# One of four sums over states accumulated by TensorE in PSUM, with a decay factor moved from PSUM to SBUF

## The chip, the cores and the metric

The kernel runs on one core of one Trainium2 chip. The metric is device time in microseconds (us) of one execution, and the number given for a kernel is the median of its runs. Everything is in fp32.

## The reference, cut to what matters

The program computes four residual layers over 2 x 2048 tokens of width 256. The change touches only the first one, a state-space (Mamba) layer; a mixture of experts, a channel mix, an attention and a second mixture of experts follow it and stay as they are.

```python
xm, z = split(x @ W_in.T)                 # ED = 512 channels each
xc    = silu(conv(xm) + conv_b)
dt, Bm, Cm = split(xc @ W_xproj.T)        # Bm and Cm have N = 16 states
delta = softplus(dt @ W_dt.T + b_dt)
dA    = exp(delta[..., None] * A)         # the decay factor, per channel and state
dBx   = delta[..., None] * Bm * xc[..., None]
h     = dA_t * h + dBx_t                  # a scan over time, per channel and state
y     = einsum('ben,bn->be', h, C_t)      # the sum over the 16 states
y     = (y + D_skip * xc) * silu(z);  out = y @ W_out.T
```

The change concerns the last sum: for every token and channel, 16 products of h and C are added up.

## The kernel before, in words

The state-space stage (`mamba_phase`) works through 8 blocks of T = 512 tokens ("units"), two to a pass of a hardware loop (`hf` = 0 and 1). In a unit the loop `for n in range(NS)` goes over the 16 states. Channels lie on partitions, in EC = 4 groups of 128; time is the free dimension. One step n of one unit, which the text calls **state n**, is:

- POOL: two `product` instructions (L400) make dBx for state n+1 in the buffer `hs[(n+1) % 4]`, 128x1024 each.
- ACT: four `factor` instructions (L554) make the decay factors of state n+1, one channel group each, in the PSUM banks `dA0` to `dA3`.
- DVE: four `scan` instructions (L778) run h = dA * h + dBx over time, reading the bank `dA[c]` and the SBUF tile `hs`, and writing h into `hs`.
- PE: four `turn`s (L924) of four 128x128 transposes each bring h of state n-1 into two PSUM banks `hT_ps` (token tile j = 0 and 2 in the one, 1 and 3 in the other), so that tokens lie on partitions and C is a number per partition.
- The four token tiles are four running sums `acc[:, j, :]` of 128x512. Tiles 0 and 2 are summed by DVE straight from PSUM (`summed`, L743). Tiles 1 and 3 (`OFF`) go another way: ACT scales them into the SBUF tile `part` (`weighted`, L568) and POOL adds `part` to `acc` (`add`, L412).

Work of state n's `turn`, `weighted`, `summed` and `add` belongs to h of state n-1: the last sum of a unit is finished in state 0 of the next. What a unit needs besides is put between the turns by two tables written by hand: `EARLY[n]` stands between turn 1 and turn 2 of state n on PE, `LATE[n]` after turn 3. Among these tasks are `y0` to `y3` of the unit before (`output`, L843 and L845, which read `acc`), `o0`, `o1`, the convolution `xc0` to `xc3` of the next unit (states 3 to 8), `dt` (state 9), `d0` to `d3` (10 and 11), `z0` to `z3` (11 to 13) and the router `r` (14). Each engine takes its instructions in order; semaphores tie them together. A wait on PE or ACT therefore holds all that stands behind it. All eight PSUM banks are taken: four `dA`, two `hT_ps`, and `fx` and `fy` for the tasks.

## Time and profile before

| | us |
|---|---|
| median of 3 runs | 2560.29 |
| lowest and highest run | 2547.91 and 2561.58 |
| the profiled execution, its own time | 2548.84 |
| span of its trace | 2547.0 |
| busy: PE, DVE, POOL, ACT | 1965.9, 1714.8, 1429.0, 1149.4 |
| mean granted TensorE clock | 0.844 |

The state-space stage takes about the first 1200 us of the span and repeats itself every 136.5 us, once for a unit. Everything below is read from one unit in the middle (about 354 to 490 us), whose picture returns in the others. The trace gives for a group of instructions its busy time and the mean of one; a timeline merges equal instructions that follow one another; where an engine sat idle, brackets give for how long and what ended it. One fp32 matmul is two matmul records.

### The profile page before, as it was taken

What the parts mean: (1) busy time and instruction counts of PE and PEld (TensorE: products, weight loads), DVE (VectorE), ACT (ScalarE), POOL (GpSimd) and SP (SyncE); (2) the same over time, 40 slices, a digit from 0 to 9 for tenths busy, and PEclk for the clock granted to TensorE, in tenths of its full rate; (3) what the DMA queues carried; (4) which work ended last, traced back from release to release, by engine and by line L of the source; (5) the groups of instructions that cost most, each with busy time, mean ns of one, the idle gap of its engine ahead of it and who ended that gap; (6) DMA issues with size and microseconds to landing.
All of it is one profiled execution on the core that took longest, in us unless ns stands there. A gap on an engine that the chain in (4) does not pass through costs nothing. (4 is left out here: it accounts for less than half of the span.)

```text
span 2547.0 us, 35987 instructions
## 1 busy us (share of the span) xinstructions
PE 1965.9 (77%) x10324; PEld 1506.0 (59%) x10325; DVE 1714.8 (67%) x3375; ACT 1149.4 (45%) x1895; POOL 1429.0 (56%) x1002
## 2 busy tenths in 40 slices
PE   6787868696978787786499999904978986599980
PEld 2445555454645454545399999803665665499970
DVE  1788788888888888885744444376943786644438
ACT  2676767677676867673223232212501442111112
POOL 1789899999989898985133333221300220255542
PEclk9897879696978888786599999956987887699995
DMA  2111111111111010111411111151000002222216
GB/s 73 34 34 47 34 47 34 46 34 44 38 34 44 28 52 30 50 34 34 205 48 48 47 47 47 39 178 35 0 17 11 9 25 90 107 71 69 69 55 197
DMA packets 77371, 139.14 MB, mean 55 GB/s; under 512 B 10449, under 2 KB 48465, under 8 KB 76450
## 3 DMA queue, kind: packets, MB, share of 16 engines
q1 hardware_dynamic: 63586, 100.19, 11.7%
q0 software_dynamic: 13632, 37.24, 4.6%
q8 instruction: 55, 0.90, 0.1%
q14 instruction: 98, 0.80, 0.1%
HBM read 105.38 MB, written 32.01 MB: 54 GB/s over the span
## 5 line engine op out<-in xcount | busy, mean ns | idle before, releaser
L778 DVE TENSOR_TENSOR_SCAN a_hs<-a_dA,a_carry,a_hs 128x512 f32<-128x512 f32 x512 | 637.1, 1268 | 27.8 <-POOL a_hs L400 23.8
L400 POOL TENSOR_TENSOR a_hs<-a_u,a_b_bc 128x1024 f32<-128x1024 f32 x258 | 625.2, 2426 | 0.4
L924 PE MATMUL a_h_ps<-k_ident,a_hs 128*128 128x128 f32 x2064 | 341.1, 318 | 184.5 <-DVE a_hs L778 113.7
L924 PEld LDWEIGHTS a_h_ps<-k_ident,a_hs 128*128 128x128 f32 x2064 | 284.6, 165 | 303.4 <-DVE a_hs L778 136.5
L554 ACT ACTIVATE a_dA<-a_delta,a_a_neg 128x512 f32<-128x512 f32 x512 | 351.7, 688 | 105.5 <-DVE a_hs L778 103.1
L412 POOL TENSOR_TENSOR a_acc<-a_acc,a_part 128x512 f32<-128x512 f32 x242 | 324.4, 1341 | 70.2 <-ACT a_part L568 69.0
L743 DVE SCALAR_TENSOR_TENSOR a_acc<-a_h_ps,a_c_tok,a_acc 128x512 f32<-128x512 f32 x242 | 177.3, 733 | 110.7 <-PE a_h_ps L924 110.6
L568 ACT ACTIVATE a_part<-a_h_ps,a_c_tok 128x512 f32<-128x512 f32 x242 | 165.7, 685 | 149.4 <-PE a_h_ps L924 133.2
L1224 POOL DMA_INDIRECT expert_rows<-m0e_ys,k_pair x71 | 74.1, 1044 | 236.2 <-DVE m0e_ys L1280 225.1
L1290 DVE TENSOR_TENSOR m0e_hT<-m0e_gs,m0e_u 128x512 f32<-128x512 f32 x70 | 48.1, 688 | 186.9 <-ACT m0e_gs L1243 186.9
L1243 ACT ACTIVATE m0e_gs<-m0e_g 128x512 f32<-128x512 f32 x71 | 42.4, 597 | 269.7 <-PE m0e_u L1321 269.7
L1247 ACT ACTIVATE m1e_hT<-m1e_u 128x512 f32<-128x512 f32 x71 | 42.4, 597 | 227.5 <-PE m1e_u L1321 227.5
L859 PE MATMUL a_fx<-a_hT,a_w_x 128*128 128x512 f32 x288 | 135.5, 606 | 7.9 <-ACT a_halo L490 7.9
L1270 DVE TENSOR_SCALAR m1e_xT<-m1e_x,k_ln_w,k_ln_b 128x128 f32<-128x128 f32 x142 | 51.7, 406 | 132.4 <-PE m1e_x L1309 119.7
L1321 PE MATMUL m1e_u<-m1e_xT,m1e_wu 128*128 128x128 f32 x1136 | 140.2, 277 | 0.5 <-DVE m1e_wu L1274 0.4
L1321 PE MATMUL m0e_g<-m0e_xT,m0e_wg 128*128 128x128 f32 x1136 | 140.1, 277 | 0.0
L1321 PE MATMUL m0e_u<-m0e_xT,m0e_wu 128*128 128x128 f32 x1136 | 139.5, 276 | 0.0
L1321 PEld LDWEIGHTS m1e_u<-m1e_xT,m1e_wu 128*128 128x128 f32 x1136 | 134.1, 194 | 1.2 <-issue 1.1
L1331 PE MATMUL m0e_y<-m0w_down,m0e_hT 128*128 x568 | 134.5, 380 | 0.2 <-DVE m0e_ys L1280 0.2
L1321 PEld LDWEIGHTS m0e_g<-m0e_xT,m0e_wg 128*128 128x128 f32 x1136 | 134.2, 194 | 0.1
L1331 PE MATMUL m1e_y<-m1w_down,m1e_hT 128*128 x568 | 134.2, 379 | 0.0
L1321 PEld LDWEIGHTS m0e_u<-m0e_xT,m0e_wu 128*128 128x128 f32 x1136 | 133.7, 193 | 0.0
(427 smaller groups left out, 3785.1 us busy)
## 6 DMA issues: line engine op xcount, KB each, us to landing
a_b_bc<-b_rows SPq DMA_DIRECT2D x132, 256.0 KB, 3.1
q_y<-expert_rows SPq DMA_DIRECT2D x32, 512.0 KB, 5.6
a_xl<-in_L_attn_x SPq DMA_DIRECT2D x9, 512.0 KB, 3.4
norm_rows<-a_shared SPq DMA_DIRECT2D x9, 512.0 KB, 2.9
m0w_up<-in_m_up SPq DMA_DIRECT2D x1, 4096.0 KB, 12.3
m0w_gate<-in_m_gate SPq DMA_DIRECT2D x1, 4096.0 KB, 22.2
m0w_down<-in_m_down SPq DMA_DIRECT2D x1, 4096.0 KB, 32.3
q_xl<-in_L_attn_x SPq DMA_DIRECT2D x8, 512.0 KB, 3.5
```

Source lines behind the costliest of these rows:

```text
L400: pool.tensor_tensor(hs[n % NBUF][:, half, :], u[s][:, half, :], b_bc[:, n % NBUF:n % NBUF + 1, :].broadcast_to([P, 2, T]), ALU.mult).then ...
L412: pool.tensor_tensor(acc[s][:, j, :], acc[s][:, j, :], part[:, j // 2, :], ALU.add).then_inc(s_add, 1)
L554: act.activation(dA[c][:], delta[s][:, c, :], ACT.Exp, scale=a_neg[:, c, k:k + 1]).then_inc(s_da, 1)
L568: act.activation(to, hT_ps[j % 2][:], ACT.Copy, scale=c_tok[s][:, j, k:k + 1]).then_inc(s_part, 1)
L743: dve.scalar_tensor_tensor(out=acc[s][:, j, :], in0=hT_ps[j % 2][:], scalar=weight, in1=acc[s][:, j, :], op0=ALU.mult, op1=ALU.add).then_i ...
L778: dve.tensor_tensor_scan(hs[k][:, c, :], dA[c][:], hs[k][:, c, :], carry[:, hf, c, n:n + 1], ALU.mult, ALU.add).then_inc(s_scan, 1)
L859: last = pe.matmul(ps[:], w_x[:, q, d, k * P:(k + 1) * P], hT[:, d, q:q + T], start=q == 0 and d == 0, stop=q == KC - 1 and d == DC - 1)
L924: last = pe.transpose(hT_ps[j % 2][:, c * P:(c + 1) * P], hs[(n - 1) % NBUF][:, c, j * P:(j + 1) * P], ident[:])
L1224: pool.indirect_dma_start(io["expert_rows"], bass.IndirectOffsetOnAxis(ap=per.pair[:, s:s + 1], axis=0), ys[s % 2][:], None).then_inc(s_st ...
L1270: last = dve.tensor_scalar(xT[k][:, c, :], x_ps[:, c, :], scale[:, c:c + 1], shift[:, c:c + 1], ALU.mult, ALU.add)
L1321: last = pe.matmul(ps[k][:, f, :], w[k][:, c, f * P:(f + 1) * P], xT[k][:, c, :], start=c == 0, stop=c == DC - 1)
L1331: last = pe.matmul(y_ps[k][:], hT[k][:, c, :], w_down[:, c, bass.ds(e * D, D)], start=c == 0, stop=c == FC - 1)
```

## The change

PSUM has eight banks and all were taken. The change frees one by keeping the decay factor of channel group 3 in an SBUF tile (`dA_sb`), so that the fourth scan reads two SBUF tiles. The freed bank (`sum_ps`) takes the sum of token tile 3 (`PILED`): ACT still scales the tile into `part`, but PE then multiplies `part` by the identity matrix and accumulates in the bank (`pile`, one fp32 matmul of 128x128 by 128x512 for each state), in place of POOL's `add`. Once for each unit ACT copies the finished sum into `acc` (`copy_sum`), and `y0` waits for that copy. Tile 1 (`ADDED`) stays with ACT and POOL, and POOL has one `add` in a state instead of two. Neither table of tasks is changed.

```diff
-        dA = [m.ps(f"dA{c}", [P, T]) for c in range(EC)]
+        dA = [m.ps(f"dA{c}", [P, T]) for c in range(EC - 1)] + [m.sb("dA_sb", [P, T])]
+        sum_ps = m.ps("sum", [P, ED])
...
-        ND, NO, ADDS = len(ON), len(OFF), len(OFF) * (NS - 1)
+        ND, NO, ADDS = len(ON), len(OFF), NS - 1
+        ADDED, PILED = OFF
...
             def add(U, n, j, s):
 
-                if j not in OFF or n == 1:
+                if j != ADDED or n == 1:
                     return
...
+            def copy_sum(U, s):
+
+                act.wait_ge(s_sum, piled(U, 0))
+                act.activation(acc[s][:, PILED, :], sum_ps[:], ACT.Copy).then_inc(s_sumc, 1)
+
             def weighted(U, n, j, s):
...
+                if j == PILED:
+                    act.wait_ge(s_sum, piled(U, n - 1))
+                    to = part[:, j // 2, :]
+                elif n == 1:
                     to = acc[s][:, j, :]
...
                         weighted(U, n, 1, here)
+                        if n == 1:
+                            copy_sum(U, 1 - hf)
                         factor(U, n + 1, 0, there)
...
                     if whole == "y0":
                         pe.wait_ge(s_acc, lin(U, NS * ND, 2 * ND))
-                        pe.wait_ge(s_add, lin(U, ADDS, 2 * NO))
+                        pe.wait_ge(s_add, lin(U, ADDS, 2))
+                        pe.wait_ge(s_sumc, lin(U, 1, 1))
...
+            def pile(U, n):
+
+                pe.wait_ge(s_part, part_count(U, n, PILED))
+                if n == 1:
+                    pe.wait_ge(s_sumc, lin(U, 1, 1))
+                pe.matmul(sum_ps[:], ident[:], part[:, PILED // 2, :], start=n == 1, stop=n == 0).then_inc(s_sum, 1)
...
                         turn(U, n, 0)
                         turn(U, n, 1)
+                        if n != 1:
+                            pile(U, n - 1)
                         for name in EARLY.get(n, []):
                             task(name, U, F, 1 - hf)
                         turn(U, n, 2)
                         turn(U, n, 3)
+                        if n == 0:
+                            pile(U, 0)
                         for name in LATE.get(n, []):
                             task(name, U, F, 1 - hf)
```

After the loop the last unit's sum is finished in the same way; the closing y of channel group 3 uses the bank `sum_ps`.

On PE, in a state of the convolution (state 5; a_hs0 to a_hs3 are the four buffers of h, a_h_ps the transposed tile, a_fy the bank of the convolution task), there stands before:

```order
L924 MATMUL a_h_ps0<-k_ident,a_hs0 128x128 [waits a_scan]
L924 MATMUL a_h_ps0<-k_ident,a_hs0 128x128 x3
L924 MATMUL a_h_ps1<-k_ident,a_hs0 128x128 [waits a_weighted_by_act]
L924 MATMUL a_h_ps1<-k_ident,a_hs0 128x128 x3
L859 MATMUL a_fy<-a_hT,a_w_x 128x512 x2
```

and after the change, at the same place:

```order
L945 MATMUL a_h_ps0<-k_ident,a_hs0 128x128 [waits a_scan]
L945 MATMUL a_h_ps0<-k_ident,a_hs0 128x128 x3
L945 MATMUL a_h_ps1<-k_ident,a_hs0 128x128 [waits a_weighted_by_act]
L945 MATMUL a_h_ps1<-k_ident,a_hs0 128x128 x3
L953 MATMUL a_sum<-a_part,k_ident 128x512 [waits a_weighted_by_act]
L879 MATMUL a_fy<-a_hT,a_w_x 128x512 x2
```

Nothing has moved but the pile (L953), which stands ahead of the convolution's matmuls, and the convolution, turn 2 and turn 3 come one matmul later.

On PE at the end of state 0 and in state 1, up to the task y0 (a_fy here), there stands before:

```order
L924 MATMUL a_h_ps<-k_ident,a_hs 128x128 [waits a_weighted_by_act]
L924 MATMUL a_h_ps<-k_ident,a_hs 128x128 x3
L918 REGISTER_ALU
L922 REGISTER_ALU [waits a_summed_by_dve]
L924 MATMUL a_h_ps<-k_ident,a_hs 128x128 [waits a_scan]
L924 MATMUL a_h_ps<-k_ident,a_hs 128x128 x3
L924 MATMUL a_h_ps<-k_ident,a_hs 128x128 [waits a_weighted_by_act]
L924 MATMUL a_h_ps<-k_ident,a_hs 128x128 x3
L896 ISA
L903 ISA [waits a_summed_by_dve,a_y_task_free]
L843 MATMUL a_fy<-a_xc,a_diag_d 128x512 [waits a_summed_by_pool]
```

and after the change:

```order
L945 MATMUL a_h_ps<-k_ident,a_hs 128x128 x3
L950 REGISTER_ALU
L953 MATMUL a_sum<-a_part,k_ident 128x512 [waits a_weighted_by_act]
L943 REGISTER_ALU [waits a_summed_by_dve]
L945 MATMUL a_h_ps<-k_ident,a_hs 128x128 [waits a_scan]
L945 MATMUL a_h_ps<-k_ident,a_hs 128x128 x3
L945 MATMUL a_h_ps<-k_ident,a_hs 128x128 [waits a_weighted_by_act]
L945 MATMUL a_h_ps<-k_ident,a_hs 128x128 x3
L916 ISA
L923 ISA [waits a_summed_by_dve,a_y_task_free]
L924 ISA [waits a_summed_by_pool]
L863 MATMUL a_fy<-a_xc,a_diag_d 128x512 [waits a_sum_copied]
```

Between turn 3 of state 0 and turn 0 of state 1 there is now a pile that waits for ACT's `weighted` of that very state, and y0 waits for ACT's copy as well.

On POOL, in one state, there stands before (a_hs is the product, a_acc the add):

```order
L400 TENSOR_TENSOR a_hs<-a_u,a_b_bc 128x1024 [waits a_b_loaded0]
L407 REGISTER_ALU
L411 REGISTER_ALU [waits a_weighted_by_act]
L412 TENSOR_TENSOR a_acc<-a_acc,a_part 128x512 [waits a_summed_by_pool]
L400 TENSOR_TENSOR a_hs<-a_u,a_b_bc 128x1024
L407 REGISTER_ALU
L411 REGISTER_ALU [waits a_weighted_by_act]
L412 TENSOR_TENSOR a_acc<-a_acc,a_part 128x512 [waits a_summed_by_pool]
```

and after the change:

```order
L409 TENSOR_TENSOR a_hs<-a_u,a_b_bc 128x1024 [waits a_b_loaded0]
L416 REGISTER_ALU
L420 REGISTER_ALU [waits a_weighted_by_act]
L421 TENSOR_TENSOR a_acc<-a_acc,a_part 128x512 [waits a_summed_by_pool]
L409 TENSOR_TENSOR a_hs<-a_u,a_b_bc 128x1024
```

The second add is gone, and the two products of neighbouring states follow each other directly.

## Rows read from the trace of the kernel before

**Rows 1.** The page's costliest groups (busy us, mean ns of one, idle before).

```profile
L778 DVE TENSOR_TENSOR_SCAN a_hs<-a_dA,a_carry,a_hs 128x512 f32<-128x512 f32 x512 | 637.1, 1268 | 27.8 <-POOL a_hs L400 23.8
L400 POOL TENSOR_TENSOR a_hs<-a_u,a_b_bc 128x1024 f32<-128x1024 f32 x258 | 625.2, 2426 | 0.4
...
L554 ACT ACTIVATE a_dA<-a_delta,a_a_neg 128x512 f32<-128x512 f32 x512 | 351.7, 688 | 105.5 <-DVE a_hs L778 103.1
...
L568 ACT ACTIVATE a_part<-a_h_ps,a_c_tok 128x512 f32<-128x512 f32 x242 | 165.7, 685 | 149.4 <-PE a_h_ps L924 133.2
```

**Rows 2.** Busy time by stretch: states 6, 10, 11, 12 and 15.

```profile
403.12:410.02 6.90, 6.90 (x30) 3.92 (x29) 6.12 (x7) 4.42 (x8) 6.90 (x5) 1.00 0.10 36
...
435.53:443.30 7.77, 4.51 (x23) 2.70 (x22) 7.73 (x16) 5.95 (x11) 7.72 (x5) 0.96 0.13 44
443.30:453.80 10.50, 10.50 (x29) 5.71 (x28) 6.22 (x8) 9.53 (x14) 6.01 (x5) 0.54 0.09 28
453.80:465.83 12.03, 6.91 (x32) 3.95 (x30) 12.03 (x11) 10.16 (x15) 11.57 (x8) 0.89 0.09 22
...
483.49:490.60 7.11, 3.85 (x18) 3.14 (x16) 6.34 (x9) 4.05 (x7) 7.11 (x5) 0.50 0.24 84
```

The columns are the stretch, its length, busy us (and count) of PE, PEld, DVE, ACT and POOL, the granted clock, the DMA share and GB/s.

**Rows 3.** Timeline of PE in state 6 (start, us, engine).

```profile
402.48 1.04 PE L924 MATMUL a_h_ps<-k_ident,a_hs 128*128 128x128 f32 x8
403.35 1.88 PE L859 MATMUL a_fx<-a_hT,a_w_x 128*128 128x512 f32 x4
405.07 1.04 PE L924 MATMUL a_h_ps<-k_ident,a_hs 128*128 128x128 f32 x8
405.94 3.60 PE L859 MATMUL a_fx<-a_hT,a_w_x 128*128 128x512 f32 x8
409.38 1.04 PE L924 MATMUL a_h_ps<-k_ident,a_hs 128*128 128x128 f32 x8
```

**Rows 4.** Timeline of POOL in the same state.

```profile
406.08 2.36 POOL L400 TENSOR_TENSOR a_hs<-a_u,a_b_bc 128x1024 f32<-128x1024 f32 x1
408.40 1.27 POOL L412 TENSOR_TENSOR a_acc<-a_acc,a_part 128x512 f32<-128x512 f32 x1
409.62 2.36 POOL L400 TENSOR_TENSOR a_hs<-a_u,a_b_bc 128x1024 f32<-128x1024 f32 x1
...
413.16 2.37 POOL L400 TENSOR_TENSOR a_hs<-a_u,a_b_bc 128x1024 f32<-128x1024 f32 x1
```

**Rows 5.** What PE waited for in the stage (us in total, times, longest).

```profile
PE a_fy L843 <- POOL a_acc L412: 22.2, 8, 3.2
```

**Rows 6.** Timeline of PE from state 0 to y0.

```profile
359.81 2.30 PE L924 MATMUL a_h_ps<-k_ident,a_hs 128*128 128x128 f32 x8 [2.23 <-DVE a_hs L778]
364.62 2.08 PE L843 MATMUL a_fy<-a_xc,a_diag_d 128*128 128x512 f32 x2 [2.51 <-POOL a_acc L412]
```

**Rows 7.** Timeline of ACT over the same stretch.

```profile
360.28 0.66 ACT L568 ACTIVATE a_part<-a_h_ps,a_c_tok 128x512 f32<-128x512 f32 x1
...
362.23 0.69 ACT L568 ACTIVATE a_acc<-a_h_ps,a_c_tok 128x512 f32<-128x512 f32 x1
```

**Rows 8.** Timeline of PE in state 11.

```profile
443.84 2.07 PE L872 MATMUL a_fx<-a_dbc,a_w_dt 64*128 64x512 f32 x2
445.71 1.91 PE L872 MATMUL a_fy<-a_dbc,a_w_dt 64*128 64x512 f32 x2
447.55 1.97 PE L924 MATMUL a_h_ps<-k_ident,a_hs 128*128 128x128 f32 x8
```

**Rows 9.** DVE operations with two SBUF inputs (ns, min/median/max).

```profile
L684 DVE SCALAR_TENSOR_TENSOR a_acc<-a_acc,a_u x18: 1196/2290/2395, 68.5 to 1139.3; 128x1024 f32<-128x1024 f32 x18
```

**Rows 10.** POOL's add over the stage (ns, min/median/max).

```profile
L412 POOL TENSOR_TENSOR a_acc<-a_acc,a_part x242: 1254/1272/2353, 87.1 to 1177.8; 128x512 f32<-128x512 f32 x121
```

**Rows 11.** Timeline of POOL in state 12.

```profile
455.77 2.21 POOL L412 TENSOR_TENSOR a_acc<-a_acc,a_part 128x512 f32<-128x512 f32 x1
457.95 3.32 POOL L400 TENSOR_TENSOR a_hs<-a_u,a_b_bc 128x1024 f32<-128x1024 f32 x1
```

**Rows 12.** Timeline of DVE in state 12.

```profile
455.66 3.41 DVE L684 SCALAR_TENSOR_TENSOR a_acc<-a_acc,a_u 128x1024 f32<-128x1024 f32 x2
```

More of the change, by code:

```diff
@@ L227, in mamba_phase @@
         s_add = m.sem("summed_by_pool")
+        s_sum = m.sem("summed_by_pe")
+        s_sumc = m.sem("sum_copied")
         s_carry = m.sem("carry")
@@ L286, in part_count, with piled @@
             return lin(U, NS * NO, NO * n + OFF.index(j) + 1 + NO)
+        def piled(U, n):
+            return lin(U, NS, n + 2)
         def added_count(U, n, j):
-            return lin(U, ADDS, NO * (n - 1 if n > 1 else 0) + OFF.index(j) + 1 + NO)
+            return lin(U, ADDS, (n - 1 if n > 1 else 0) + 2)
         ROWS = R + 2 * NS
         N_WEIGHTS = 16 * 11
-        N_PREP = 1 + EC + 8
+        N_PREP = 1 + EC + 9
         PER_D = 2 * (2 + 2)
@@ L370, in _ @@
             pool.memset(xc[1][:], 0.0).then_inc(s_prep, 1)
+            pool.memset(part[:, PILED // 2, :], 0.0).then_inc(s_prep, 1)
             pool.memset(H[:, BT - TJ:BT, :], 0.0).then_inc(s_prep, 1)
-            pool.sem_inc(s_add, NO)
+            pool.sem_inc(s_add, 1)
             pool.wait_ge(s_const, 2)
@@ L408, in add @@
                 if n == 0:
-                    pool.wait_ge(s_add, added_count(U, 0, j) + -NO)
+                    pool.wait_ge(s_add, added_count(U, 0, j) + -1)
                 elif n > 2:
@@ L446, in _ @@
             end = (0, 2 * NB, None)
-            for j in OFF:
-                add(end, 0, j, 1)
+            add(end, 0, ADDED, 1)
             rms(TILES - TJ, lambda per_: per_ * (2 * NB + 1))
@@ L561, in weighted @@
                 k = (n - 1) % NS
-                if n == 1:
+                if n == 1 and j == OFF[0]:
                     act.wait_ge(s_free[side("ct")], count("ct", before(U)))
+                if j == PILED:
+                    act.wait_ge(s_sum, piled(U, n - 1))
+                    to = part[:, j // 2, :]
+                elif n == 1:
                     to = acc[s][:, j, :]
                 else:
-                    act.wait_ge(s_add, added_count(U, 0, j) + -NO if n == 0 else added_count(U, n - 1, j))
+                    act.wait_ge(s_add, added_count(U, 0, j) + -1 if n == 0 else added_count(U, n - 1, j))
                     to = part[:, j // 2, :]
@@ L651, in _ @@
                 weighted(end, 0, j, 1)
+            copy_sum(end, 1)
             act.wait_ge(s_free["Y"], len(FSEQ["Y"]) + 2 * NB * len(SEQ["Y"]) + 2)
@@ L823, in _ @@
                 dve.wait_ge(s_yl, c + 1)
-                dve.tensor_tensor(z[1][:, c, :], dA[c][:], z[1][:, c, :], ALU.mult).then_inc(s_yg, 1)
+                dve.tensor_tensor(z[1][:, c, :], (dA[0:EC - 1] + [sum_ps])[c][:], z[1][:, c, :], ALU.mult).then_inc(s_yg, 1)
             t_end = TILES - TJ
@@ L932, in _ @@
             pe.wait_ge(s_prep, N_PREP)
+            pe.matmul(sum_ps[:], ident[:], z[1][:, 0, :], start=True, stop=False)
             with pe.Fori(0, NB) as i:
@@ L948, in _ @@
                 turn(end, 0, j)
+                if j == 1:
+                    pile(end, -1)
+            pile(end, 0)
             pe.wait_ge(s_acc, lin(end, NS * ND, 2 * ND))
-            pe.wait_ge(s_add, lin(end, ADDS, 2 * NO))
+            pe.wait_ge(s_add, lin(end, ADDS, 2))
+            pe.wait_ge(s_sumc, 2 * NB + 1)
             pe.wait_ge(s_da, 2 * NB * NS * EC + EC)
+            last_y = dA[0:EC - 1] + [sum_ps]
             for c in range(EC):
-                output(dA[c], c, 1).then_inc(s_yl, 1)
+                output(last_y[c], c, 1).then_inc(s_yl, 1)
             pe.wait_ge(s_yg, EC)
```

## Prediction

> **What bounds the kernel now.** I read the page's costliest groups first, then a table of busy times by state for one unit, then the timelines of PE, POOL, DVE and ACT in the states that the table singled out. The groups [rows 1] show POOL's two products at 2.4 us each and DVE's four scans at 1.27 us as the largest work of the stage; that alone suggests that POOL, which also has two adds, sets the pace. The table [rows 2] says more. In state 6, one of the convolution's, POOL is busy for 6.90 of 6.90 us, but so is PE, at a granted clock of 1.00, while DVE has 6.12. State 15 has POOL full (7.11 of 7.11), PE at 3.85. State 11 has PE full (10.50 of 10.50) and POOL at 6.01. State 12 has DVE full (12.03). So the bound changes inside a unit, and an add taken from POOL is worth something only in the states where POOL alone is full: 15, 0 and half of 14. The reader is to see in the timeline of PE [rows 3] that in a convolution state turn, matmul, turn, matmul stand back to back with no wait in brackets: 402.48 to 409.38 is 6.90 us, the length of the state. States 4 to 8 look so.
>
> **What is removed.** One add of 1.27 us, which takes 1.22 us of POOL's sequence (408.40 to 409.62 [rows 4]). POOL's state is 7.08 us (406.08 to 413.16 [rows 4]) and becomes 5.86. Where POOL alone is the bound the next limit is DVE, 6.34 us in state 15 [rows 2]: at most 0.74 us a state, 2.5 states, 1.8 us a unit. PE's wait for POOL's last add ahead of y0 goes too: 22.2 us in 8 units, 2.8 each [rows 5]; what takes its place is worked out below.
>
> **The pile in states 4 to 8.** It is one fp32 matmul of 128x512, two records. Four such records fill 403.35 to 405.07 [rows 3], 0.43 us each, so a pile is 0.86 us of a full PE. Nothing covers it: PE has no wait in these states. From 6.90 a state goes to 7.76, while POOL falls below. Five states: **+4.3 us a unit**. Elsewhere (states 2, 3, 9, 10, 12, 13, 15) PE waits between its turns and the pile lies in that wait; without this cover each would cost 0.86 us too.
>
> **States 0 and 1.** The pile after turn 3 of state 0 waits for ACT's `weighted` of the same turn. In the trace that one runs late, 360.28 to 360.94 [rows 7], because four layer-norm instructions stand ahead of it on ACT. The turns of state 1 started at 359.81 [rows 6]. Behind the waiting pile they now start after 360.94 and a pile. The clock is 0.50 here (state 15 in [rows 2]); at such a clock two records take 1.87 us (443.84 to 445.71 [rows 8]). So: pile done at 362.8, eight transposes of 1.97 [rows 8] to 364.8, `weighted` 0.7, the copy 0.7 (nearest row: the same shape from PSUM, 685 ns [rows 1]), y0 at 366.4, against 364.62 [rows 6]: **+1.8 us a unit**. Bounds: at the full clock (0.86 for the pile, 1.04 for the turns [rows 3]) y0 starts at 364.4, -0.2; if DVE's sum of state 1, behind the delayed turn 0, decides instead, the whole shift of the turns, 362.8 less 359.81, +3.0.
>
> **State 11.** PE is full, at a clock of 0.54 [rows 2], and ACT's evacuation of d2 and d3 waits for it. The pile stands ahead of d2: **+1.9 us a unit** by [rows 8], 0.9 at the full clock.
>
> **The fourth scan and the SBUF port.** Scans with dA in PSUM have one SBUF tensor input and show no disturbance: their mean is 1268 ns beside a busy POOL [rows 1]. No scan of this kernel reads two SBUF tiles, so its behaviour beside POOL has to be bounded from other operations. DVE's scalar_tensor_tensor with two SBUF inputs has a minimum of 1196 ns and a median of 2290 [rows 9]: 1.09 us is waiting. At the same moment (two of them, 455.66 for 3.41 us [rows 12]) POOL's add takes 2.21 us instead of 1.27 and its product 3.32 instead of 2.36 [rows 4, 10, 11], each 0.95 us longer. Each engine waits for the other's instruction to end. The fourth scan should do this in every state: it waits up to 1.1 us for POOL, and POOL loses 1.27 less the 0.25 that the pairs overlap (1.20 against 0.95), 1.0 us. In a state where POOL is full its 5.86 becomes 6.87, against 7.08: the gain is 0.2 and not 0.74, over 2.5 states **-0.5 us a unit**. In states 2, 10, 12, 13 and 14 DVE or what waits for it decides, and scan 3 is followed by turn 0 of the next state; there the wait counts. POOL is busy for 7.72 of 7.77 us in state 10 and 11.57 of 12.03 in state 12 [rows 2], with less to do after the change; I take 0.6 us, about half of the 1.09 seen: **+3.0 us a unit**. Bounds: 0 if the scan takes no port from POOL, 5.5 if it waits for 1.09 in each. In states 4 to 8 DVE has 0.8 us to spare now and 1.6 then, which hides the wait.
>
> The Trainium skill, page "SBUF — State Buffer", section "Who interferes with whom", says that VectorE with two SBUF inputs and GpSimd take one shared pair of ports by an exclusive lock, each for the whole instruction. By that rule, the stretched pairs agree, and it speaks against moving the factor to SBUF; without it the unit would be 4.3 us shorter than with it (3.0 less the wait, 1.3 more relief).
>
> **ACT.** Writing the factor to SBUF costs nothing by the rows: 688 ns into PSUM, 685 from PSUM into SBUF [rows 1]. The page "ScalarE: Activation LUTs" of the Trainium skill, section "Step-by-step: what each stage is for", calls ScalarE's way to PSUM the faster one; the two rows do not show it, and the sum leaves it out. The copy adds 0.7 us a unit, counted above.
>
> **Sum.** 4.3 + 1.8 + 1.9 + 3.0 - 0.5 = 10.5 us a unit, 84 us in 8 units. The profiled execution took 2548.84 us, so 2633. The median of the runs stands 11 us above the profiled one and a new median may fall anywhere in that spread; I say **2637**.
>
> **The rivals.**
> - **The scan takes no port.** For it: no scan in the trace shows a lock. Against it: two other operations with two SBUF inputs behave alike. 4.3 + 1.8 + 1.9 - 1.8 = 6.2 a unit, +50: 2598. Chance 0.20.
> - **The clock rises in the slow states.** PE has more to do in states 13 to 1 and in 9 to 11, and the clock may stay at 1.00. For it: the clock is 1.00 in the full states 4 to 8. Against it: it is at 0.54 in state 11 although PE is busy throughout. 4.3 - 0.2 + 0.9 + 3.0 - 0.5 = 7.5 a unit, +60: 2609. Chance 0.15.
> - **Faster: POOL is what sets the pace in the convolution states, and PE has hidden room.** POOL is full there as well [rows 2], and a busy PE is modelled. If PE takes the pile into gaps that the records do not show, and the scan takes no port, the states with a full POOL (4 to 8, 14, 15, 0, 2) fall toward DVE's 6.34: 9 x 0.7 = 6.3 us a unit, -50: 2498. It decides only where a pile in states 4 to 8 costs less than the 0.18 us by which POOL's 7.08 stands above PE's 6.90. Against it: [rows 3] leaves no gap. Chance 0.06.
> - **Nothing measurable.** The port costs little, the clock rises and POOL's relief pays for the convolution states; about 2560. Chance 0.06.
> - **Worse.** The waits for the port chain up: 4.3 + 3.0 + 1.9 + 5.5 = 14.7 a unit, +118: 2666 or more. Chance 0.08 for what lies near or above.
> My own forecast keeps 0.45.
>
> **How the numbers follow.** Lowest bound of each term without a port: 4.3 - 0.2 + 0.9 - 1.8 = 3.2 a unit, +26 us, 2575; highest 2666, and 11 us for the spread of the medians. The range is 2583 to 2672: it leaves out the faster and the unchanged case (0.12) and the ends of the others. A measurement of this kernel can tell about 0.5%, 13 us, from no change. Faster 0.06, same 0.06, slower 0.88.
>
> **What the changed kernel's profile would show.** Right: in states 4 to 8 PE stays full and the state takes 7.7 to 7.8 us, not 6.9; turns of state 1 start about 3 us later against the fourth scan of state 0; the scan that reads the SBUF factor has a mean well above 1268 ns and POOL's products have a maximum of 3.3 us in many states, not only in 12 and 13; a unit takes 147 us, not 136.5. Wrong: a fourth scan of 1.27 us throughout; waits on PE in the convolution states; a granted clock above 0.9 in states 13 to 1; POOL still without idle time in states 4 to 8. The prediction fails upward if DVE waits for POOL in states that I hold to be covered (4 to 9), and downward if the pile is hidden there.

## The result, and the profile after

| | before | after |
|---|---|---|
| median (20 runs each) | 2556.61 us | 2567.70 us |
| lowest to highest | 2547.91 to 2565.89 | 2560.44 to 2581.96 |
| profiled execution, span | 2548.84, 2547.0 | 2570.06, 2568.3 |
| mean granted clock over the span | 0.844 | 0.883 |

The ratio is 1.0050 with a 95% interval of 1.0034 to 1.0065: slower by about 13 us, at the edge of what was called measurable. The forecast was 2637 with a range of 2583 to 2672; the result lies below its range.

The page's costliest groups of after (busy us, mean ns of one, idle before), against [rows 1]:

```profile
L409 POOL TENSOR_TENSOR a_hs<-a_u,a_b_bc 128x1024 f32<-128x1024 f32 x258 | 683.5, 2667 | 1.0 <-issue 0.3
L798 DVE TENSOR_TENSOR_SCAN a_hs<-a_dA,a_carry,a_hs 128x512 f32<-128x512 f32 x384 | 479.8, 1264 | 11.8 <-POOL a_hs L409 8.5
...
L421 POOL TENSOR_TENSOR a_acc<-a_acc,a_part 128x512 f32<-128x512 f32 x121 | 186.8, 1544 | 130.9 <-ACT a_part L585 130.2
...
L798 DVE TENSOR_TENSOR_SCAN a_hs<-a_dA_sb,a_carry,a_hs 128x512 f32<-128x512 f32 x128 | 247.0, 1930 | 0.0
```

Three quarters of the scans are as they were; the fourth takes 1930 ns in the mean, and POOL's product went from 2426 to 2667. POOL now has 130 us of idle time in which it waits for ACT: over the stage as a whole it no longer sets the pace.

PE in state 6 (timeline: start, us), against [rows 3]:

```profile
408.99 1.04 PE L945 MATMUL a_h_ps<-k_ident,a_hs 128*128 128x128 f32 x8
409.86 1.02 PE L953 MATMUL a_sum<-a_part,k_ident 128*128 128x512 f32 x2
410.72 1.88 PE L879 MATMUL a_fx<-a_hT,a_w_x 128*128 128x512 f32 x4
412.44 1.03 PE L945 MATMUL a_h_ps<-k_ident,a_hs 128*128 128x128 f32 x8
413.31 3.60 PE L879 MATMUL a_fx<-a_hT,a_w_x 128*128 128x512 f32 x8
416.75 1.03 PE L945 MATMUL a_h_ps<-k_ident,a_hs 128*128 128x128 f32 x8
```

408.99 to 416.75 is 7.76 us where it was 6.90: the pile's 0.86 us, in full. Busy time by stretch in after (columns as in [rows 2]): states 0, 1, 4, 11 and 12.

```profile
360.01:368.77 8.76, 5.92 (x18) 3.42 (x17) 6.99 (x7) 5.96 (x11) 8.76 (x5) 0.69 0.26 92
368.77:378.39 9.62, 8.27 (x52) 6.19 (x51) 9.02 (x17) 5.05 (x12) 6.16 (x4) 0.94 0.20 55
394.10:401.87 7.77, 7.77 (x32) 4.31 (x31) 6.87 (x7) 4.56 (x8) 6.76 (x4) 1.00 0.10 34
...
451.45:461.31 9.86, 9.21 (x31) 4.44 (x30) 7.26 (x7) 7.32 (x12) 6.86 (x4) 0.81 0.14 34
461.31:473.82 12.51, 8.35 (x36) 4.44 (x36) 12.16 (x11) 12.45 (x17) 8.47 (x6) 1.00 0.06 21
```

State 11, all at 0.54 in [rows 2], is at 0.81 now, and at 1.00 from the middle on: the timeline of PE there, against [rows 8]:

```profile
450.30 1.97 PE L945 MATMUL a_h_ps<-k_ident,a_hs 128*128 128x128 f32 x8 [2.63 <-DVE a_hs L798]
452.06 1.92 PE L953 MATMUL a_sum<-a_part,k_ident 128*128 128x512 f32 x2
453.90 1.77 PE L892 MATMUL a_fx<-a_dbc,a_w_dt 64*128 64x512 f32 x2
455.52 1.02 PE L892 MATMUL a_fy<-a_dbc,a_w_dt 64*128 64x512 f32 x2
```

The pile takes 1.92 us, as forecast; but the clock rises behind it, and the second pair of d takes 1.02 instead of 1.91.

One unit's states differ, so all are compared by one measure: the length of a state from DVE's first sum in it to the first sum of the next, worked out from the timelines of DVE as a mean over units 1 to 6 of 8 (us), and the mean granted clock of the same stretches. The kernels below "after" are those of the experiments: "small outside" has piles of 4 columns outside states 4 to 8, "pairs" is the kernel before with an idle pair in all states, "no port" is that without POOL's second add, "ring" has three banks in rotation, and "fastest" is the last one. Where a state of another kernel is quoted below, it is by the same measure. A clock of 1.00 is 2.4 GHz and one of 0.50 is 1.2 GHz; values between are a mean over both levels.

```
state           unit     0     1     2     3   4-7     8     9    10    11    12    13    14    15
before         136.5  6.68 12.68  8.84  6.86  6.90  8.64  9.78  7.78  9.94 12.49 10.21  7.46  7.52
after          138.3  8.26  9.45  8.88  6.87  7.76  9.50  8.60  8.11  9.87 12.26 10.26  7.78  7.36
factor alone   147.5  8.09 12.78  8.85  7.16  8.00  8.29 10.44  8.69 10.25 13.31 10.47  9.03  8.12
small outside  143.9  7.56 11.45  9.32  7.88  7.69  9.50 10.56  9.05 10.62 11.93 10.15  7.98  7.17
pairs          139.8  6.80 12.78  8.86  8.07  7.76  9.50  8.60  7.78  7.72 13.42 10.18  7.49  7.61
no port        133.2  6.21  9.72  8.85  8.06  7.76  9.50  9.09  7.78  7.72 11.20 10.17  6.44  7.46
ring           138.2  8.27  9.26  8.86  6.86  7.76  9.50  8.60  7.78 11.37 11.67 11.39  6.38  7.28
ring, pair     134.8  8.16  9.65  8.87  6.87  7.76  9.50  9.99  7.77  8.12 10.94 10.21  6.33  7.32
after, pair    142.2  8.02 10.54  8.95  6.88  7.76  9.50  9.75  9.59 10.13 12.33 10.27  7.75  7.42
fastest        130.3  8.32  9.96  8.90  6.86  6.90  8.64  9.46  7.77  8.11 10.94 10.24  6.30  7.17
clock before    0.83  0.50  0.72  1.00  1.00  1.00  1.00  0.86  0.96  0.57  0.91  0.77  0.54  0.50
clock after     0.93  0.72  0.98  1.00  1.00  1.00  1.00  1.00  0.95  0.79  0.96  0.89  0.78  0.74
```

The unit grew by 1.8 us where 10.5 were forecast. States 4 to 8 give +4.3, as forecast; state 0 has +1.6, and states 1 and 9 give back 3.2 and 1.2.

### The profile page after: what moved, and what is told of

It reads as the page before. It is cut to its first block and busy times, and to the rows that moved or that the text cites. A ratio compares the mean times of both kernels' runs of the same rounds, so it can differ in the third digit from the quotient of the medians.

```text
span 2568.3 us, 36192 instructions
## 1 busy us (share of the span) xinstructions
PE 2018.7 (79%) x10586; PEld 1502.8 (59%) x10587; DVE 1788.3 (70%) x3375; ACT 1155.8 (45%) x1904; POOL 1383.0 (54%) x882
## 5 line engine op out<-in xcount | busy, mean ns | idle before, releaser
L409 POOL TENSOR_TENSOR a_hs<-a_u,a_b_bc 128x1024 f32<-128x1024 f32 x258 | 683.5, 2667 | 1.0 <-issue 0.3
L798 DVE TENSOR_TENSOR_SCAN a_hs<-a_dA,a_carry,a_hs 128x512 f32<-128x512 f32 x384 | 479.8, 1264 | 11.8 <-POOL a_hs L409 8.5
L945 PEld LDWEIGHTS a_h_ps<-k_ident,a_hs 128*128 128x128 f32 x2064 | 262.7, 153 | 284.2 <-DVE a_hs L798 146.4
L945 PE MATMUL a_h_ps<-k_ident,a_hs 128*128 128x128 f32 x2064 | 307.6, 297 | 144.5 <-DVE a_hs L798 113.9
L562 ACT ACTIVATE a_dA<-a_delta,a_a_neg 128x512 f32<-128x512 f32 x384 | 264.6, 689 | 58.1 <-DVE a_hs L798 56.5
L421 POOL TENSOR_TENSOR a_acc<-a_acc,a_part 128x512 f32<-128x512 f32 x121 | 186.8, 1544 | 130.9 <-ACT a_part L585 130.2
L585 ACT ACTIVATE a_part<-a_h_ps,a_c_tok 128x512 f32<-128x512 f32 x250 | 171.3, 685 | 175.2 <-PE a_h_ps L945 170.6
L798 DVE TENSOR_TENSOR_SCAN a_hs<-a_dA_sb,a_carry,a_hs 128x512 f32<-128x512 f32 x128 | 247.0, 1930 | 0.0
L953 PE MATMUL a_sum<-a_part,k_ident 128*128 128x512 f32 x260 | 163.4, 716 | 22.7 <-ACT a_part L585 22.7
```

The lines of the kernel that those rows point to most:

```text
L409: pool.tensor_tensor(hs[n % NBUF][:, half, :], u[s][:, half, :], b_bc[:, n % NBUF:n % NBUF + 1, :].broadcast_to([P, 2, T]), ALU.mult).then ...
L421: pool.tensor_tensor(acc[s][:, j, :], acc[s][:, j, :], part[:, j // 2, :], ALU.add).then_inc(s_add, 1)
L562: act.activation(dA[c][:], delta[s][:, c, :], ACT.Exp, scale=a_neg[:, c, k:k + 1]).then_inc(s_da, 1)
L585: act.activation(to, hT_ps[j % 2][:], ACT.Copy, scale=c_tok[s][:, j, k:k + 1]).then_inc(s_part, 1)
L798: dve.tensor_tensor_scan(hs[k][:, c, :], dA[c][:], hs[k][:, c, :], carry[:, hf, c, n:n + 1], ALU.mult, ALU.add).then_inc(s_scan, 1)
L945: last = pe.transpose(hT_ps[j % 2][:, c * P:(c + 1) * P], hs[(n - 1) % NBUF][:, c, j * P:(j + 1) * P], ident[:])
```

## The experiments

Ratios are to the kernel before, timed beside each group of kernels, with 95% intervals. Its own median moved between 2549.8 and 2556.6 us from group to group, so that a difference of medians across groups can be off by some 6 us; the ratios are not. "Pair" is an idle fp32 matmul of the pile's size, two records.

**The factor alone.** Kernel before, with only dA[3] in SBUF; both adds stay on POOL.

```diff
-        dA = [m.ps(f"dA{c}", [P, T]) for c in range(EC)]
+        dA = [m.ps(f"dA{c}", [P, T]) for c in range(EC - 1)] + [m.sb("dA_sb", [P, T])]
```

> The kernel before with one part of the change alone: the fourth decay factor is written to and read from an SBUF tile; both adds stay on POOL, PE has no pile, and the freed bank serves only as the last output's bank at the end of the stage. Theory A (the scan with two SBUF inputs and POOL exclude each other, and a full POOL pays for it): each state with a full POOL goes from 7.08 to about 8.1 us, eight such states in a unit, and 1.4 us more in the others, in all +9.4 us a unit, +75 us, ratio 1.029. Theory B (POOL and the scan find room beside each other, because POOL does not set the pace where PE is full): +1.4 us a unit as in the changed kernel, +11 us, ratio 1.004.

2639.70 us, ratio 1.0343 (1.0312 to 1.0373), +11.0 us a unit. The fourth scan beside a POOL with both adds (page, costliest groups):

```profile
L413 POOL TENSOR_TENSOR a_acc<-a_acc,a_part 128x512 f32<-128x512 f32 x242 | 402.7, 1664 | 53.7 <-ACT a_part L569 52.8
L779 DVE TENSOR_TENSOR_SCAN a_hs<-a_dA_sb,a_carry,a_hs 128x512 f32<-128x512 f32 x128 | 303.0, 2367 | 0.0
```

It takes 1.1 us longer than with its factor in PSUM, the wait of [rows 9], and POOL's adds take 1664 ns in the mean against a median of 1272 [rows 10]. So a scan with two SBUF inputs waits as those operations do, and the factor's place alone costs 3.4%, more than the 2.9% that were expected at most. That the whole change costs 0.5% means that the rest of it gains some 9 us a unit.

**Small piles.** Kernel after, with piles of 4 columns for 512, so that most of the sum of tile 3 is left out: everywhere; in states 4 to 8 alone; everywhere but there (the edit shown).

```diff
-                pe.matmul(sum_ps[:], ident[:], part[:, PILED // 2, :], start=n == 1, stop=n == 0).then_inc(s_sum, 1)
+                cols = slice(0, 4) if n != 1 and not 3 <= n <= 7 else slice(0, ED)
+                pe.matmul(sum_ps[:, cols], ident[:], part[:, PILED // 2, cols], start=n == 1, stop=n == 0).then_inc(s_sum, 1)
```

> The changed kernel with every pile cut from 512 to 4 columns (the sum of token tile 3 is left out but for 4 columns); all waits stay. Theory A (the piles keep the granted clock up outside the convolution states, and that gives back most of what they cost there): states 4 to 8 fall from 7.76 to about 7.0 us, but the clock is again near 0.83 in state 9, 0.54 in state 11 and 0.50 in 15, so that state 9 goes from 8.6 to about 10 us and state 11 stays near 10; about -2 us a unit against the changed kernel, -16 us, near the kernel before. Theory B (what the forecast counted too much was slack, not clock): every pile's time comes off, states 9 and 11 shorten too, -5.5 us a unit, -44 us, ratio 0.988 to before.

2569.42 us, ratio 1.0062 (1.0040 to 1.0083): no faster than after, with most of the pile's work gone. States 5 to 7 take 7.13 us, but state 1 takes 11.37 (9.45 in after), 9 and 10 together 18.2 (16.7).

> The changed kernel with the piles of states 4 to 8 alone cut to 4 columns (their five states are left out of the sum of tile 3 but for 4 columns). If PE's row of turns, pile and convolution sets the pace there: 7.76 us becomes 6.95 to 7.05 us in each of the five, -3.8 us a unit, -30 us against the changed kernel, ratio to before 0.993. Rival: POOL with the fourth scan on its port (5.86 plus 1.0) or a fourth scan that waits sets the pace as soon as PE is relieved, 7.3 us or more, -2 us a unit and less, -16 us.

2544.41 us, ratio 0.9958 (0.9941 to 0.9975). States 4 to 7 take 7.13 us, not 6.90: even a pile of 4 columns takes 0.2 us. The unit is 2.3 us shorter than in after, and not the 3.2 that these five states give: states 1 and 9 to 11 are 0.2 to 0.3 us longer, with the unit's clock at 0.915 for 0.926.

> The changed kernel with the piles outside states 4 to 8 cut to 4 columns, but for the first of a unit (they are left out of the sum of tile 3 but for 4 columns); the piles of states 4 to 8 stay whole. Theory A (clock): the granted clock falls back in states 10, 11, 13 to 15, 0 and 1 to what the kernel before has; y0 in state 1 is slow again (3.6 us to its reader, not 2.2), and the time stays within 6 us of the changed kernel though PE has less to do. Theory B (slack): a shorter pile in states 0 and 11 gives 2.5 us a unit, -20 us against the changed kernel.

2613.59 us, ratio 1.0244 (1.0203 to 1.0285): **46 us above after, with less work on PE**, where at most 6 were expected. State 1 has +2.0 us, 3 +1.0, 9 +2.0, 10 +0.9, 11 +0.8. The clock of the unit is 0.835 where after has 0.926. PE in state 9 there (timeline):

```profile
448.86 0.28 PE L954 MATMUL a_sum<-a_part,k_ident 128*128 128x4 f32 x2
449.43 0.66 PE L945 MATMUL a_h_ps<-k_ident,a_hs 128*128 128x128 f32 x4 [0.29 <-DVE a_acc L763]
452.65 1.11 PE L945 MATMUL a_h_ps<-k_ident,a_hs 128*128 128x128 f32 x4 [2.57 <-ACT a_part L585]
453.56 6.10 PE L887 MATMUL a_fy<-a_xc,a_w_proj 128*96 128x512 f32 x8
```

and the same operations in after:

```profile
434.88 1.02 PE L953 MATMUL a_sum<-a_part,k_ident 128*128 128x512 f32 x2
435.74 0.60 PE L945 MATMUL a_h_ps<-k_ident,a_hs 128*128 128x128 f32 x4
438.68 0.66 PE L945 MATMUL a_h_ps<-k_ident,a_hs 128*128 128x128 f32 x4 [2.34 <-ACT a_part L585]
439.17 3.60 PE L887 MATMUL a_fy<-a_xc,a_w_proj 128*96 128x512 f32 x8
```

The eight records of the projection take 3.60 us behind a full pile and a wait of 2.34 us, and 6.10 behind a small pile and a wait of 2.57. The pile's work in these states holds the clock up, and that is worth more than it costs.

**No port for the fourth scan.** Kernel after; the scan reads the PSUM bank of dA[2], so that channel group 3 is scanned with the factor of group 2, and ACT writes the third factor only behind it.

```diff
-                            dve.tensor_tensor_scan(hs[k][:, c, :], dA[c][:], hs[k][:, c, :],
+                            dve.tensor_tensor_scan(hs[k][:, c, :], dA[min(c, EC - 2)][:], hs[k][:, c, :],
```

> The changed kernel, but the fourth scan reads the PSUM bank of the third decay factor (so channel group 3 is scanned with the factor of group 2) and ACT's third factor of the next state waits for the fourth scan; ACT still writes the fourth factor to SBUF, where nobody reads it. The fourth scan has one SBUF tensor input. Expected if the port costs what the two profiles show: all scans at 1.27 us, POOL's products at 2.36 throughout, states 4 to 8 unchanged at 7.76, states 10, 12, 13, 14 shorter by 1.4 us in all and 15 and 0 by 0.5 each: -2 us a unit, -16 us against the changed kernel, ratio to before about 0.999. Rival, the forecast's size (3.0 us of waits and 1.3 us of POOL's relief a unit): -34 us, ratio 0.992. If the later third factor matters, it is seen as a wait of DVE for ACT, and the gain is smaller.

2581.58 us, ratio 1.0115 (1.0087 to 1.0143). Inconclusive on the port: states 12, 13 and 14 are shorter by 0.5, 1.2 and 1.0 us, but states 3, 9 and 11 are longer by 1.0, 2.6 and 1.3. ACT's factors wait 157 us for scans where they wait 57 in after: the later third factor is the likely cause, which no further run separates.

**The last pile of a unit, later.** Kernel after; the pile of state 0 stands behind turn 1 of state 1, as in the other states.

```diff
-                        if n != 1:
-                            pile(U, n - 1)
+                        pile(U, n - 1)
```

> The changed kernel with the last pile of a unit moved from the end of state 0 to behind turn 1 of state 1, like all others; it computes all. If that pile holds up turn 0 of state 1: PE's wait for ACT ahead of it (22.7 us in 8 units) goes, DVE's sum in state 1 starts 2 to 3 us earlier after the fourth scan of state 0, and y0 starts 0.5 to 1.5 us earlier: -1 us a unit, -8 us, ratio to before 1.002. Rival: y0 waits for ACT's copy, which now comes after the moved pile as well, so that y0 is no earlier: 0 us.

2582.38 us, ratio 1.0124 (1.0103 to 1.0145). State 0 falls by 1.4 us, as expected, and state 1 rises by 2.1, with its clock at 0.78 for 0.98; state 11 rises by 0.9 at 0.64 for 0.79. As a mean over the units y0 starts 0.4 us earlier, and what follows it in state 1 takes 1.0 us longer. Removing PE's wait was no gain.

**Pairs in the kernel before.** A pair ahead of turn 0: in states 9 to 1; the same with half of its columns; in all states.

```diff
+                if j == 0 and (n >= 9 or n <= 1):
+                    pe.matmul(hT_ps[0][:, 0:512], ident[:], w_z[:, 0, 0:512], start=True, stop=True)
```

> The kernel before with nothing of the change, but one idle matmul pair (identity by a weight tile, 512 columns) ahead of turn 0 in states 9 to 15, 0 and 1, while PE waits for the fourth scan; the turns overwrite what it writes, so the result is unchanged. Theory A (the granted clock outside the convolution states follows how much PE has to do there, and a higher clock shortens states 9, 11 and 1): clock near 0.9 over the unit against 0.83, -3 us a unit, -24 us, ratio 0.990. Theory B (the clock is only a bystander, and the states went faster by the missing add): no gain, or up to 0.6 us a state lost where the pair ends after the scan, +3 us a unit, +24 us.

2552.32 us, ratio 0.9988 (0.9972 to 1.0005): a miss. State 11 does fall by 2.2 us at clock 1.00, and 9 by 0.7, but states 3, 8 and 12 rise by 1.1, 0.9 and 0.9. The 0.9 of state 8 is the pair ahead of turn 0 of state 9: PE is full there and the pair costs its 0.86.

> As the kernel with the idle pair in states 9 to 1, with 256 columns in place of 512. By theory A the clock is raised less or not at all, a ratio between that kernel's 0.990 and 1.000; if the smaller pair raises it as well, it costs less at turn 0 and the ratio is the lowest of the four.

2562.56 us, ratio 1.0030 (1.0012 to 1.0047), above both bounds of what was expected. State 11 takes 9.6 us at clock 0.67: half a pair does not bring the clock back.

> As the kernel with the idle pair in states 9 to 1, but in all 16 states. If PE is full in states 4 to 8 the five pairs cost 0.86 us each there, 4.3 us a unit over that kernel, and the ratio to the kernel before is about 1.003 by theory A. If POOL set the pace there (7.08 against PE's 6.90), the cost is 0.7 each or less, and it shows as idle time of POOL.

2588.40 us, ratio 1.0128 (1.0102 to 1.0153): +3.3 us a unit where the same matmuls were forecast at 6.2 (4.3 and 1.9). The clock of states 9 to 12 is 1.00, and states 9 and 11 are 1.2 and 2.2 us shorter than before.

**The same without POOL's add of tile 3 and without the port.** Four factors in PSUM, a pair ahead of turn 0 in all states but 1, no copy; the sum of tile 3 is left out.

```diff
-                if j not in OFF or n == 1:
+                if j != ADDED or n == 1:
                     return
...
+                if j == 0 and n != 1:
+                    pe.matmul(hT_ps[0][:], ident[:], w_z[:, 0, :], start=True, stop=True)
```

> The change's work on PE and POOL without its layout: all four decay factors stay in PSUM, POOL's add of tile 3 is gone, and in place of the pile an idle pair of the same size stands ahead of turn 0 in all states but 1 (the sum of tile 3 is left out; ACT still scales it; there is no copy). All scans have one SBUF input. Theory A (the port costs 3.0 us a unit in states 10, 12, 13 and 14, as the kernel without it at the fourth scan shows there): -3 us a unit against the changed kernel, -24 us, ratio to before 0.996. Rival, the port costs 1.4 or less, as the difference of the two first profiles has it: ratio 1.001. Rival, the forecast's 4.3: 0.992.

2525.14 us, ratio 0.9874 (0.9845 to 0.9903), below all three that were expected. Against the kernel with pairs everywhere, at about the same clock (0.938 and 0.934), the unit is 6.6 us shorter: 3.1 in state 1, 2.2 in state 12, 1.1 in state 14, 0.6 in state 0, with state 9 0.5 longer. (The pair ahead of turn 0 of state 1 is missing too; its share of the 0.6 was not measured alone.) In state 1 it is the wait ahead of y0 that goes, with pairs everywhere and then here:

```profile
369.27 1.14 PE L843 MATMUL a_fy<-a_xc,a_diag_d 128*128 128x512 f32 x2 [2.27 <-POOL a_acc L412]
```

```profile
357.70 1.63 PE L853 MATMUL a_fy<-a_xc,a_diag_d 128*128 128x512 f32 x2
```

DVE's operation of [rows 9] in this kernel and then in after (ns, min/median/max):

```profile
L694 DVE SCALAR_TENSOR_TENSOR a_acc<-a_acc,a_u x18: 1217/1222/1226, 68.4 to 1117.3; 128x1024 f32<-128x1024 f32 x18
```

```profile
L704 DVE SCALAR_TENSOR_TENSOR a_acc<-a_acc,a_u x18: 1195/1218/2297, 68.1 to 1155.5; 128x1024 f32<-128x1024 f32 x18
```

With pairs everywhere and both adds its median is still 2294 ns. Its two waits for POOL in state 12 are gone with the add: 2 x 1.07 = 2.1 us of the 2.2.

**Three banks in rotation.** A full kernel without the port: the factors rotate over three PSUM banks, the fourth sum bank stays, and ACT writes the fourth factor behind the first weighted tile.

```diff
+        def bank(U, n, c):
+            return dA[(U[1] * NS * EC + n * EC + c) % PASS % 3]
...
                         weighted(U, n, 1, here)
-                        factor(U, n + 1, 0, there)
+                        factor(U, n, 3, hf)
```

> The changed kernel with the freed bank won in another way: the four decay factors of a state go round three PSUM banks, each written once the scan that read it three factors earlier is done, and ACT's fourth factor of a state moves behind the first scaling of that state. All scans have one SBUF tensor input; piles, copy and adds are as in the changed kernel, and all is computed. Theory A (the fourth scan's port costs 4 to 5 us a unit, as the kernel with neither port nor bank shows): the fourth scan at 1.27 us, POOL's products at 2.36, -4 us a unit against the changed kernel, -32 us, ratio to before 0.992. Rival (a later factor on ACT costs what the port gave, as in the kernel whose third factor waits for the fourth scan): DVE waits for ACT's factors, ratio 1.000 or more.

2566.71 us, ratio 1.0053 (1.0032 to 1.0074), the same as after, near the rival's figure. States 12 and 14 are 0.6 and 1.4 us shorter, as the port's removal should make them; states 11 and 13 are 1.5 and 1.1 longer, the former at clock 0.55. Then the same with tile 3 left to POOL in states 4 to 8, where PE is full, its sum brought into the bank by one pile in state 9:

```diff
+        MIX = range(3, 8)
...
-                if j != ADDED or n == 1:
+                if n == 1 or (j != ADDED and not (j == PILED and n in MIX[1:])):
```

> The kernel with three banks in turn, and tile 3 added by POOL as before in the convolution states (four adds; ACT writes the first part straight into the sum in SBUF), by PE's piles elsewhere, with one more pile in state 9 that brings POOL's part into the bank. All is computed. If PE's full row is what costs in states 4 to 8: 7.76 us becomes 7.1 (POOL's two products and two adds), -3.3 us a unit against the kernel with three banks, -26 us, ratio to before 0.982. Rival: with less to do PE's clock falls in states 9 and 11 as in the kernel with small piles in 4 to 8, which takes 1 us a unit back: 0.985.

2539.47 us, ratio 0.9940 (0.9917 to 0.9963): states 4 to 8 are at 6.90 (8.64 the last), 4.3 us less. State 11 gives 0.8 of it back: 12.17 us for 11.37, both at clock 0.55. Against the kernel with three banks alone it is 27 us, as was forecast; the ratio is above the forecast since that kernel was slower than it had been taken for.

**A pair in states 10 and 11**, in the kernel with three banks, in after, and in the last one above.

```diff
+                if j == 0 and n in (10, 11):
+                    pe.matmul(hT_ps[0][:], ident[:], w_z[:, 0, :], start=True, stop=True)
```

> The kernel with three PSUM banks in turn, and an idle matmul pair ahead of turn 0 in states 10 and 11 only, where PE waits for the fourth scan. All is computed. If the granted clock (0.55 in state 11 of that kernel) is what took back the port's gain: clock 1.00 in state 11, that state 11.4 to about 8 us, with 1 us of it moved into state 12: -2.5 us a unit against that kernel, -20 us, ratio to before 0.997. If the later factors on ACT took it back: state 11 stays above 10 us, ratio 1.005.

2535.55 us, ratio 0.9938 (0.9915 to 0.9960), a gain of 31 us over three banks alone (29 by the ratios), more than the 20 expected. PE in state 11 of the kernel without the pair:

```profile
449.07 1.11 PE L958 MATMUL a_h_ps<-k_ident,a_hs 128*128 128x128 f32 x8 [2.32 <-DVE a_hs L811]
450.00 1.89 PE L966 MATMUL a_sum<-a_part,k_ident 128*128 128x512 f32 x2
451.82 2.07 PE L905 MATMUL a_fx<-a_dbc,a_w_dt 64*128 64x512 f32 x2
453.68 1.91 PE L905 MATMUL a_fy<-a_dbc,a_w_dt 64*128 64x512 f32 x2
```

and with it:

```profile
438.70 1.12 PE L956 MATMUL a_h_ps<-a_w_z,k_ident 128*128 128x512 f32 x2 [1.12 <-DVE a_acc L776]
439.88 1.09 PE L960 MATMUL a_h_ps<-k_ident,a_hs 128*128 128x128 f32 x8
440.81 1.02 PE L968 MATMUL a_sum<-a_part,k_ident 128*128 128x512 f32 x2
441.77 1.12 PE L905 MATMUL a_fx<-a_dbc,a_w_dt 64*128 64x512 f32 x2
442.73 1.02 PE L905 MATMUL a_fy<-a_dbc,a_w_dt 64*128 64x512 f32 x2
```

The pair lies in the 2.3 us for which PE waited anyway, the clock stays at 2.4 GHz instead of 1.2, and the operations behind it take about half the time: state 11 is 8.12 us for 11.37. States 12 and 13 are 0.7 and 1.2 us shorter too, and state 9, at the end of which the first pair stands, is 1.4 longer.

> The changed kernel with the same idle pair ahead of turn 0 in states 10 and 11. All is computed. Its difference to the kernel with three banks and the same pair is the port's price at one and the same clock. Clock theory: state 11 from 9.9 to about 8.5 us, -1 us a unit, ratio 1.002, and the port's price is then 1.5 us a unit or more; if the two kernels stand within 0.2% the port costs nothing that can be measured beside the piles.

2591.37 us, ratio 1.0166 (1.0137 to 1.0195): 24 us above after, a miss. States 1, 9 and 10 are 1.1, 1.2 and 1.5 us longer, and state 11 gains nothing: there the pair does not bridge the wait.

```profile
457.30 1.12 PE L943 MATMUL a_h_ps<-a_w_z,k_ident 128*128 128x512 f32 x2 [1.12 <-DVE a_acc L763]
460.24 1.97 PE L947 MATMUL a_h_ps<-k_ident,a_hs 128*128 128x128 f32 x8 [1.81 <-DVE a_hs L798]
462.00 1.92 PE L955 MATMUL a_sum<-a_part,k_ident 128*128 128x512 f32 x2
463.85 2.07 PE L892 MATMUL a_fx<-a_dbc,a_w_dt 64*128 64x512 f32 x2
```

Behind it PE waits another 1.81 us for the scan, and the clock is at its lower level behind that wait. The two kernels with the pair differ only in the factors, their place and their turn on ACT: 7.4 us a unit and 2.3% apart, of which states 10, 11, 12 and 14 have 6.6.

> The kernel with three banks in turn and POOL's adds in the convolution states, with the same idle pair in states 10 and 11. All is computed. Clock theory: state 11 from 12.2 to about 8 us, 1 us of it moved into state 12: -3 us a unit, -24 us, ratio to before 0.985. Otherwise 0.994 as without the pair.

2503.62 us, ratio 0.9815 (0.9788 to 0.9843): the fastest of all, with nothing left out, 1.9% below the kernel before.

## Why the prediction missed

**Direction and ladder.** Slower was right, the size was not, and the direction is no merit of the whole sum: states 4 to 8 were right with +4.3, and all the rest, forecast at +6.2, came to -2.5. The runs split the change in three steps, in us a unit: PE's matmuls, +3.3 (before to pairs); one add less on POOL, -6.6 (pairs to no port); the port, the pile's waits and the copy, +5.0 (no port to after). With rounding this is the +1.8 of the traces. For the same steps the forecast holds +6.2; -4.6 (1.8 of relief and the 2.8 of y0's wait); and +8.9 (the port, the relief that it takes away, and what the pile of state 0 and the copy put in the place of y0's wait).

Of the 8.7 us missed, 4.7 are the clock's (states 9 and 11, and state 1 behind y0), 1.9 lie ahead of y0, and 2.1 in the relief of the states in which the port counts.

**States 4 to 8, +4.3: right**, to the hundredth; with small piles there most of it goes (7.76 to 7.13).

**State 11, +1.9: the clock's step failed.** The pile takes 1.92 us as said, yet the state is 0.1 us shorter, and state 9, which the sum held at nothing, 1.2 shorter. Every price was taken at the clock of the kernel before. The sentence against the rival, that the clock is at 0.54 in state 11 although PE is busy throughout, was misread: PE had gone into that state from a wait. This is the row ahead of [rows 8]:

```profile
442.27 1.64 PE L924 MATMUL a_h_ps<-k_ident,a_hs 128*128 128x128 f32 x8 [2.32 <-DVE a_hs L778]
```

With pairs everywhere, in the same place:

```profile
450.27 1.12 PE L922 MATMUL a_h_ps<-a_w_z,k_ident 128*128 128x512 f32 x2 [1.13 <-DVE a_acc L743]
451.47 1.09 PE L926 MATMUL a_h_ps<-k_ident,a_hs 128*128 128x128 f32 x8
452.49 1.12 PE L872 MATMUL a_fx<-a_dbc,a_w_dt 64*128 64x512 f32 x2
```

State 11 is 7.7 us there for 9.9, at clock 1.00: a bridge over the wait undoes the low clock. The rival with 0.15 was right in its mechanism; its price was wrong too, since it only made the added work cheaper, and not the work that stood there before.

**What is removed, -1.8, cut to -0.5: state 12 was left out.** Measured -6.6, at about equal clocks. Of it 1.8 us lie in states 14, 15 and 0, the sum that the forecast had for them, though more in 14 and less in 15; 3.1 lie in state 1, which the forecast saw as 2.8 [rows 5] and set against the delay of the pile; 2.2 lie in state 12, and it had the rows for them [rows 11, 12]: two DVE operations that each wait 1.1 us for POOL's add. They were read as a model of what the fourth scan would pay, not as a wait that ends when the add is taken away. The rule that POOL's relief counts only where POOL alone is full was the fault: a wait for POOL in a state that DVE bounds counts as well.

**States 0 and 1, +1.8: measured -1.7.** The delay of state 0 is there (+1.6; PE waits for the pile's data, longest 4.0 us, 22.7 in total):

```profile
PE a_sum L953 <- ACT a_part L585: 22.7, 9, 4.0
...
PE a_fy L863 <- ACT a_acc L567: 10.8, 8, 1.4
```

The wait of y0 for the copy is 1.4 us at most, against 2.8 in [rows 5], and that offsets the delay: as a mean over units 1 to 6 y0 starts 10.1 us after the first sum of state 0, and 10.2 in the kernel before. (The forecast's own terms, 362.8, eight transposes, 0.7 and 0.7, give 366.2 and not the 366.4 written, +1.6.) The other 1.5 us come behind y0, where nothing was forecast: from y0 to state 2 it is 7.6 us for 9.1, with the clock of state 1 at 0.98 for 0.72. This is the clock again. With small piles outside of states 4 to 8, one add and the copy as in after, but a clock of 0.70, it is 9.4. The rows of y0 there and in after:

```profile
381.37 2.07 PE L863 MATMUL a_fy<-a_xc,a_diag_d 128*128 128x512 f32 x2 [1.35 <-ACT a_acc L567]
383.23 1.91 PE L865 MATMUL a_fy<-k_ident,a_acc 128*128 128x128 f32 x8
```

```profile
370.83 1.12 PE L863 MATMUL a_fy<-a_xc,a_diag_d 128*128 128x512 f32 x2 [1.35 <-ACT a_acc L567]
371.80 1.05 PE L865 MATMUL a_fy<-k_ident,a_acc 128*128 128x128 f32 x8
```

That state 1 is shorter by about 3 us both here and in the kernel without port is chance: there it is nearly all y0's wait, at a clock of 0.83; here it is about half the wait and half the clock.

**The port, +3.0: right in mechanism and about in size, but not seen in the net.** From no port to after, states 10, 12, 13 and 14 have +0.3, +1.1, +0.1 and +1.3, 2.8 us, and state 2 none; with three banks in rotation states 10, 12 and 14 give 2.3 of it back. The net from before to after is +0.5 in these four, since the relief in 12 and 14 pays for the rest. The rival without a port is out. The Trainium skill, "SBUF — State Buffer", section "Who interferes with whom", says that a VectorE instruction with two SBUF inputs and a GpSimd instruction that reads SBUF contend by an exclusive lock. The 1930 and 2367 ns of the fourth scan, against 1264 for its neighbours, agree.

**ACT, nothing:** in after, factors into SBUF take a median of 722 ns and those into PSUM 685: 0.04 us each, 5 us over 128 if nothing hid them, which the sum left out. The two rows by which the forecast held this at nothing compare different instructions.

**Left open.** The price of the port at one and the same clock: the two kernels with the pair in states 10 and 11 differ by 7.4 us a unit, but at 0.939 and 0.901, so that part of it is the clock's; from no port to after the clock falls too, and state 11 alone is 2.1 us longer. Why states 3 and 12 grow when pairs are put ahead of turn 0 was not tried. The pairs show that a low clock goes with an unbridged wait of PE, but the length of the wait alone does not tell: 2.34 us in state 9 of after leave it at its upper level, 1.81 us in state 11 of after with the pair do not. The cases between (half a pair, the pile of state 0 moved) were not forecast well by anything that I had.

## What to carry to other kernels

Price a change at the clock that it will itself leave, both ways: matmuls put where TensorE waits can cost nothing and speed up all behind them, and work taken away there can cost (46 us here). They can also gain nothing: pairs in nine states of the kernel before left it at 0.9988, and a pair with a wait left behind it cost 24 us. Ask of each slow state which wait stands ahead of it, and try it. Matmuls added to a row of TensorE without waits cost their full time. When an operation is taken off GpSimd, look for VectorE operations with two SBUF inputs beside it: their waits can end too, even where GpSimd is not the bound (2.2 us in state 12). And do not move an input of a VectorE operation from PSUM to SBUF beside a full GpSimd (3.4% here).
